# Query and key products of a two-stage attention: Strassen blocks of two heads by two batches in place of two heads by two halves of one batch

## The reference, cut to what matters

```python
qh = (q_in @ wq + bq).reshape(b, q_len, H, K)      # H = 16, K = 128, b = 4, q_len = 256, D = 256
kh = (kv_in @ wk + bk).reshape(b, t, H, K)         # kv_in is the same context in both
vh = (kv_in @ wv + bv).reshape(b, t, H, K)
kh = jnp.concatenate([kh, jnp.broadcast_to(bias_k, (b, 1, H, K))], axis=1)   # 257 keys
vh = jnp.concatenate([vh, jnp.broadcast_to(bias_v, (b, 1, H, K))], axis=1)
scale = jnp.sqrt(jnp.asarray(K, q_in.dtype))
logits = jnp.einsum('bqhk,bthk->bhqt', qh, kh) / scale
weights = jax.nn.softmax(logits, axis=-1)
ctx = jnp.einsum('bhqt,bthk->bqhk', weights, vh).reshape(b, q_len, H * K)
return ctx @ wo + bo
```

## Time and profile before

| what | us |
|---|---|
| median of 3 runs | 1529.41 (1529.25 to 1532.53) |
| the profiled execution, its own time | 1532.75 |
| its span, first to last instruction | 1529.90 |
| first wide stage | 258.76 to 634.94 |
| second wide stage | 634.94 to 1012.92 |
| TensorE / VectorE / ScalarE / GpSimd busy | 1460.5 / 978.5 / 938.6 / 208.2 |
| mean granted TensorE clock | 0.995 |

### The profile page before, as it was taken

One profiled execution on the slowest core, in us unless ns is written; L12 is line 12 of the kernel. 1 busy time (PEld: TensorE's weight loads), 2 busy tenths in 40 slices (PEclk: granted clock), 3 DMA queues, 4 the chain that ended last, 5 costly groups with the idle time before them and its releaser, 6 DMA issues.

```text
span 1529.9 us, 30796 instructions
## 1 busy us (share of the span) xinstructions
PE 1460.5 (95%) x10544; PEld 1144.6 (75%) x10544; DVE 978.5 (64%) x3454; ACT 938.6 (61%) x3047; POOL 208.2 (14%) x283
## 2 busy tenths in 40 slices
PE   7999999999999999999999999999899998999997
PEld 5766678888888888778878888878666666866664
DVE  4777822565565656556556665631899996158997
ACT  5878933544454444344445444533899997379996
POOL 2010042010010102201000010011222322012200
PEclk9999999999999999999999999999999999999999
DMA  7000002010010100101001000000100100000000
GB/s 297 1 2 2 35 31 80 32 39 26 1 62 3 49 16 1 63 1 49 16 1 63 1 1 1 7 9 1 56 2 9 36 16 8 1 1 9 16 2 22
DMA packets 10891, 40.79 MB, mean 27 GB/s; under 512 B 2417, under 2 KB 2673, under 8 KB 8689
## 3 DMA queue, kind: packets, MB, share of 16 engines
q1 hardware_dynamic: 10736, 38.82, 7.0%
HBM read 37.77 MB, written 1.05 MB: 25 GB/s over the span
## 4 chain that ended last, share of the span: by engine, by line
PE 64%; ACT 18%; issue 5%; DVE 2%; POOL 1%; POOLq 0%; DVEq 0%; ACTq 0%
ACT probs L1094 11%; PE bank L908 8%; PE bank L876 7%; PE bank L889 7%; PE bank L922 7%; PE bank L853 7%; PE bank L866 5%; PE bank L797 5%; ACT pT L1102 5%; PE bank L786 5%; PE bank L897 4%; PE bank L631 2%; PE bank L615 1%; PE bank L937 1%; ACT hT L1050 1%
## 5 line engine op out<-in xcount | busy, mean ns | idle before, releaser
L1094 ACT ACTIVATE probs<-probs,negmax 128x256 f32<-128x256 f32 (+1 forms) x640 | 351.8, 567 | 41.2 <-DVE negmax L1378 40.5
L1170 ACT ACTIVATE pT<-bank,cols 128x128 f32<-128x128 f32 x480 | 151.3, 372 | 247.0 <-PE bank L853 247.0
L631 PEld LDWEIGHTS bank<-ident,probs 128*128 128x128 f32 x1536 | 167.6, 141 | 119.5 <-ACT probs L1094 60.6
L631 PE MATMUL bank<-ident,probs 128*128 128x128 f32 x1536 | 226.1, 280 | 28.8 <-ACT pT L1102 17.5
L1378 DVE CUSTOM_DVE_ANT_0 probs<-bank,mask_a 128x256 f32<-128x256 f32 (+1 forms) x384 | 173.9, 509 | 28.5 <-PE bank L615 23.7
L1102 ACT ACTIVATE pT<-bank 128x512 f32<-128x512 f32 x288 | 172.9, 602 | 6.7 <-PE bank L631 6.6
L1523 DVE TENSOR_REDUCE stats<-bank 128x1 f32<-128x257 f32 x256 | 108.5, 425 | 74.7 <-PE bank L889 73.8
L1569 DVE TENSOR_TENSOR pT<-bank,pT 128x256 f32<-128x256 f32 x180 | 76.0, 422 | 118.4 <-PE bank L866 118.4
L1188 ACT ACTIVATE pT<-bank 128x512 f32<-128x512 f32 x128 | 76.5, 598 | 122.1 <-PE bank L897 122.1
L908 PE MATMUL bank<-pT,probs 128*128 128x256 f32 x512 | 139.9, 396 | 4.3 <-ACT pT L1188 4.1
L1094 ACT ACTIVATION_READ_ACCUMULATOR probs<-probs,negmax 128x1 f32 x640 | 138.1, 216 | 0.0
(11 more groups left out here) (198 smaller groups left out, 2680.0 us busy)
## 6 DMA issues: line engine op xcount, KB each, us to landing
w_m<-in_w SPq DMA_DIRECT2D x6, 1024.0 KB, 6.9
g_qkv<-in_g SPq DMA_DIRECT2D x4, 1536.0 KB, 6.8
q_res<-in_g SPq DMA_DIRECT2D x4, 1536.0 KB, 6.4
w_qkv<-in_w SPq DMA_DIRECT2D x3, 768.0 KB, 4.3
g_bv<-in_gbv SPq DMA_DIRECT2D x8, 256.0 KB, 6.7
g_o<-in_go SPq DMA_DIRECT2D x4, 512.0 KB, 3.4
q_res<-in_go SPq DMA_DIRECT2D x4, 512.0 KB, 3.2
rows<-in_rows SPq DMA_DIRECT2D x1, 1664.0 KB, 14.0
```

The costliest lines, as they stand in the source:

```text
L631: last = nc.tensor.transpose(out[:, n * P:(n + 1) * P], probs[:, u % PROBS, q * T + t * P:q * T + (t + 1) * P], ident[:, :])
L1094: last = nc.scalar.activation(s, s, ACT.Exp, bias=negmax[:, u % PROBS, k:k + 1], scale=-1.0, accum_out=sums[:, tile % 2, q, j * c.res + r: ...
L1170: last = nc.scalar.activation(to[:, w, :], bank[KQ_BANK][:, w * P:(w + 1) * P], ACT.Identity, bias=col(("bq", "bk")[w] + str(j), at))
```

## The change

A block is now two heads by two batches. Its halves in the third direction are two whole batches of 256 columns, where they were two halves of 128 columns of one batch. A block still has 7 products for query and 7 for key, each now 256 columns wide, and makes four heads-of-a-batch. There are 16 blocks a stage, of which two (8 heads-of-a-batch, `DIRECT`) are plain `kq`. Block steps run in rows 1 to 56, one step a row: in three rows of four `add_r1` and `add_r2` together ahead of `times_v`, in one row `add_r1` alone; none at the row's end. ScalarE reads one whole bank a row, VectorE adds one whole bank in three rows of four, behind `outputs(n)`. The ring has twelve places: five in pT, seven in `v_two`, which is therefore zeroed again behind the stages. `c_sum`'s second part lies in `w_qkv[0]`, so the load of that tile moves to the end of the second stage. The diff, cut to its core:

```diff
...
-PAIRS = HEADS // 2
-DIRECT = 4
...
+BLOCKS = HEADS // 4
+DIRECT = 8
...
-        qk1 = pT[:, 4:9, :].rearrange("p a t -> p (a t)")[:, 0:4 * (T + K1)].rearrange("p (n t) -> p n t", n=4)
-        h_sum = [m[:, i, :].rearrange("p (s t) -> p s t", s=4) for m in (mask_a, mask_m) for i in range(2)]
-        n = 4 * K1 + 2048
-        c_sum = [v_four[:, i, :, :, :].rearrange("p a b c -> p (a b c)") for i in range(2)] + [
-            pT[:, 9, :], flat[:, n:n + 512]]
-        c_sum = [x.rearrange("p (s t) -> p s t", s=4) for x in c_sum]
+        wide = [pT[:, 4:10, :].rearrange("p a t -> p (a t)"), v_two[:, :, :, :, :].rearrange("p a t r d -> p (a t r d)")]
+        qk1 = [wide[i >= 5][:, (i - 5 * (i >= 5)) * (T + K1):(i - 5 * (i >= 5) + 1) * (T + K1)] for i in range(12)]
+        h_sum = [m[:, :, :].rearrange("p i t -> p (i t)") for m in (mask_a, mask_m)]
+        c_sum = [v_four[:, :, :, :, :].rearrange("p i a b c -> p (i a b c)"),
+                 w_qkv[0][:, :, :, :].rearrange("p w k d -> p (w k d)")[:, 0:4 * T]]
+        h_sum, c_sum = [[x.rearrange("p (s t) -> p s t", s=4) for x in y] for y in (h_sum, c_sum)]
         q_all = g_qkv[0][:, :, :, :].rearrange("p w k d -> p (w k d)")[:, 0:2 * KT * T]
         q_all = q_all.rearrange("p (x i t) -> p x i t", x=2, i=KT)
...
+        def steps_in(n):
+            c = (n - 1) // 4 + DIRECT // 4
+            return (c, (n - 1) % 4) if n >= 1 and c < BLOCKS else None
+        def block_of(n):
+            u, h = divmod(n, H1)
+            return u // 2 * 2 + h // 2, (h % 2) * 2 + u % 2
+        def qk_of(n):
+            c, at = block_of(n)
+            return qk1[c % 3 * 4 + at]
...
-            load(w_qkv[0][:, :, :, :], a["w_2c"], "s_w0")
...
-            sp.wait_ge(sem("b_r1"), end("b12", "b_r1"))
+            sp.wait_ge(sem("b_r2"), end("b12", "b_r2"))
+            load(w_qkv[0][:, :, :, :], a["w_2c"], "s_w0")
...
-                    out = bank[SUM_BANK if n == 2 else KQ_BANK]
+                    out = bank[SUM_BANK if n >= 2 and n % 2 == 0 else KQ_BANK]
                     if n == 0:
                         weights("c_qkv", g, 16)
-                        rows_turned(pe, before, b)
                         pe.wait_ge(sem("b_r1out"), st.at("b_r1out", 0))
                     elif n == 2:
                         pe.wait_ge(sem("b_r2out"), st.at("b_r2out", 0))
-                    pe.wait_ge(sem("b_kq"), st.at("b_kq", 0, n - 1 if n == 3 else n if n < 2 else 1))
+                    if h == 0:
+                        rows_turned(pe, before, b)
+                    pe.wait_ge(sem("b_kq"), st.at("b_kq", 0, n - 1 if n >= 3 else min(n, 1)))
                     for k in range(KT):
                         mm(out[:, 0:T], g_qkv[g % 2][:, 1, k, h * P:(h + 1) * P], ctxT[:, b, k, :],
...
+                def blocks(c, w):
+                    g, bp, x, _ = block_at(c)
                     src = ctxT if w else hT
-                    return (lambda h, k: g_qkv[g % 2][:, w, k, at[h]], lambda s: w_sum[:, x, s - 1, w, :],
-                            lambda k, t: src[:, b, k, t * P:(t + 1) * P],
-                            lambda s: (c_sum if w else h_sum)[b][:, s - 1, :])
...
+                def add_r1(c, step):
+                    g, bp, x, i = block_at(c)
                     pe.wait_ge(sem("b_r1out"), st.at("b_r1out", 0, 4 * i + step))
                     if step == 0 and i == 0:
                         pe.wait_ge(sem("b_kq"), st.at("b_kq", 0, DIRECT))
-                    if step == 0 and b == 0 and x == 0:
+                    if step == 0 and bp == 0 and x == 0:
                         weights("c_qkv", g, 16)
                     if step == 0 and g == 0 and x == 0:
-                        rows_turned(pe, before, b)
+                        rows_turned(pe, before, 2 * bp)
                     if step == 1:
                         pe.wait_ge(sem("b_wsum"), st.at("b_wsum", 0, 2 * g + x + 1))
-                        pe.wait_ge(sem("b_hsum"), st.at("b_hsum", 0, B if g else b + 1))
+                        pe.wait_ge(sem("b_hsum"), st.at("b_hsum", 0, B // 2))
                         if i == 0:
-                            pe.wait_ge(sem("b_csum"), B)
+                            pe.wait_ge(sem("b_csum"), B // 2)
                     for w in range(2):
-                        wt, ws, xt, xs = blocks(m, w)
+                        wt, ws, xt, xs = blocks(c, w)
                         one, two = [(wt(0, 0), xt(0, 0)), (ws(2), xs(2)), (ws(3), xs(3)), (wt(1, 1), xs(4))][step]
-                        last = mm(bank[KQ_BANK][:, w * P:(w + 1) * P], one, two, start=(step == 0 and w == 0),
+                        last = mm(bank[KQ_BANK][:, w * T:(w + 1) * T], one, two, start=(step == 0 and w == 0),
                                   stop=(step == 3), skip_group_check=True)
                     last.then_inc(sem("b_r1"), 1)
...
+                def add_r2(c, step):
+                    i = block_at(c)[3]
                     pe.wait_ge(sem("b_r2out"), st.at("b_r2out", 0, 3 * i + step))
                     if step == 0 and i == 0:
                         pe.wait_ge(sem("b_kq"), st.at("b_kq", 0, DIRECT))
                     for w in range(2):
-                        wt, ws, xt, xs = blocks(m, w)
+                        wt, ws, xt, xs = blocks(c, w)
                         one, two = [(wt(0, 1), xt(1, 0)), (ws(1), xs(1)), (ws(4), xt(1, 1))][step]
-                        last = mm(bank[SUM_BANK][:, w * P:(w + 1) * P], one, two, start=(step < 2 and w == 0),
+                        last = mm(bank[SUM_BANK][:, w * T:(w + 1) * T], one, two, start=(step < 2 and w == 0),
                                   stop=(step != 1), skip_group_check=True)
                     last.then_inc(sem("b_r2"), 1)
...
-                        i = pair(n // 2)[3]
-                        pe.wait_ge(sem("b_r1out"), st.at("b_r1out", 0, 4 * (i + 1)))
-                        pe.wait_ge(sem("b_r2out"), st.at("b_r2out", 0, 3 * (i + 1)))
+                        c, at = block_of(n)
+                        i = block_at(c)[3]
+                        if at == 2:
+                            pe.wait_ge(sem("b_r1out"), st.at("b_r1out", 0, 4 * (i + 1)))
+                        else:
+                            pe.wait_ge(sem("b_r2out"), st.at("b_r2out", 0, 3 * i + (1, 3, None, 2)[at]))
...
-                kq(2)
-                kq(3)
+                for n in range(2, DIRECT):
+                    kq(n)
                 for n in range(HEADS):
-                    m = n // 2 + DIRECT // 2
                     u, h = divmod(n, H1)
                     if n + 1 < HEADS:
                         scores(n + 1)
...
-                    if n % 2 == 0:
-                        if n and m <= PAIRS:
-                            add_r2(m - 1, 2)
-                        if m < PAIRS:
-                            add_r1(m, 0)
-                    elif m < PAIRS:
-                        add_r1(m, 2)
-                        add_r2(m, 1)
+                    if steps_in(n):
+                        c, step = steps_in(n)
+                        add_r1(c, step)
+                        if step != 1:
+                            add_r2(c, max(step - 1, 0))
...
-                    if m < PAIRS:
-                        if n % 2 == 0:
-                            add_r1(m, 1)
-                            add_r2(m, 0)
-                        else:
-                            add_r1(m, 3)
...
+                def read_r1(c, step):
+                    g, bp, x, i = block_at(c)
                     act.wait_ge(sem("b_r1"), st.at("b_r1", 0, 4 * i + step + 1))
                     h, t = [(0, 0), (0, 1), (1, 1), (1, 0)][step]
...
+                    to, at = qk1[c % 3 * 4 + 2 * h + t], g * H1 + 2 * x + h
+                    nc.scalar.activation(to[:, 2 * T:T + K1], col(f"key{j}", at), ACT.Copy)
                     for w in range(2):
-                        last = nc.scalar.activation(to[:, w, :], bank[KQ_BANK][:, w * P:(w + 1) * P], ACT.Identity,
-                                                    bias=col(("bq", "bk")[w] + str(j), at))
+                        last = nc.scalar.activation(to[:, w * T:(w + 1) * T], bank[KQ_BANK][:, w * T:(w + 1) * T],
+                                                    ACT.Identity, bias=col(("bq", "bk")[w] + str(j), at))
                     last.then_inc(sem("b_r1out"), 1)
...
+                    if steps_in(n):
+                        read_r1(*steps_in(n))
...
+                    if c.host and p == 0:
+                        dve.wait_ge(sem("s_zero"), 3)
...
+                    to = qk1[c % 3 * 4 + (0, 3, 1)[step]][:, 0:2 * T]
+                    v.tensor_tensor(to, bank[SUM_BANK][:, :], to, ALU.add).then_inc(sem("b_r2out"), 1)
...
-                    if n and n % 2 == 0 and m <= PAIRS:
-                        add_r2(m - 1, 2)
...
+                    if steps_in(n):
+                        c, step = steps_in(n)
+                        if step != 1:
```

(79 more changed lines are left out.)

32 lines of the change are left out of this document (7 added, 25 removed).

## The result

The changed kernel takes 1520.2 us (median of 4 runs, 1520.17 to 1520.21); the kernel before took 1529.6 beside it (4 runs, 1529.25 to 1532.53). The ratio is 0.9933, with a 95% interval from 0.9921 to 0.9945. The forecast was 1521.5, with a range from 1517.0 to 1526.5. The profiled execution took 1520.21 with a span of 1518.4; the forecast for a profiled execution was 1524.8, from 1532.75 before.

The account below looks back on a forecast made before the run. Each stage was taken to last as long as TensorE's list. The terms summed to -7.9 us, taking the kernel's own 1532.75 to 1524.8; the median of the runs shown is 3.3 lower, so 1521.5, range 1517.0 to 1526.5.

Parts of the forecast that it names:

- Step products: TensorE's step records in both stages: fewer, 256-column records at 0.2156 us each, plus four more `kq`; -4.0 us.
- The wait for the turned block: 36 rows a stage: more step work behind the turns removes 0.07 us of waiting for ScalarE's copy; -5.0 us.
- rows with one sum: Rows h = 2, with `add_r1` alone: 0.03 us of saved step work returns as a wait in 28 rows; +0.8 us.
- VectorE before `values`: Rows h = 2: VectorE's `add_r2` no longer precedes the value add, so TensorE's second `values` stops waiting; -1.9 us.
- Row 0: First row: falls from 5.68 to 3.13 us, with its 12 step records counted elsewhere; -2.4 us.
- Rows 57 to 59: Both stages' rows left without step work: 0.96 us idle behind the turns in place of 0.07; +5.3 us.
- Row 60: Loses four records behind the turns and waits as much longer; +0.8 us.
- GpSimd, -1.5: Ahead of stage one: two 256-column `c_sum` replace four, shortening TensorE's 3.01 us idle before the next norm; -1.5 us.
- The clock: Falls to 1.2 GHz, about 1.7 us each: first may go (-1.7), both stage ends get thinner (+1.7 each); let cancel.
- Rival 5: Slower: `SUM_BANK` drained too late by VectorE, each of 112 step rows paying the excess; 1538 at 0.15 a row; chance 0.06.

Follow-up runs that it names:

- step_records_of_128: Changed kernel with every 256-column step product issued as two records of 128 columns, in both sums; 1527.2 us, ratio 0.9976.
- r2_at_row_end: Changed kernel with TensorE's second sum (`add_r2`) moved from behind the turned block to the row's end; 1527.9 us, ratio 0.9982.
- late_second_sum: Changed kernel with the last block's `add_r2` of steps 1 and 2 moved from rows 55 and 56 to 57 and 58; 1516.9 us, ratio 0.9911.
- late_sum_and_norm: Changed kernel with the last block's two late `add_r2` moved two rows later and GpSimd's next norm ahead of its second weight sum; 1515.9 us, ratio 0.9906.
- extra_adds_beside_none: Changed kernel with two needless VectorE adds ahead of each real one, only for a block's first and second sums; 1520.6 us, ratio 0.9935.
- norm_before_weights: Changed kernel with GpSimd's power and bias of the next norm ahead of stage one's second weight sum; 1518.55 us, ratio 0.9923.

## Why the prediction was right

It was right by its terms, not by luck between them; the sum for the two stages without the clock was -6.4 (-7.9 less GpSimd's -1.5), and the stages show -3.16 and, with the fall taken out, -3.4: together -6.6.

- **Step products, -4.0.** Records start 0.216 apart, as the nearest rows had it, and the unit of four rows went from 22.15 to 21.69 where 22.1 and 21.6 were forecast. `step_records_of_128` puts 2.54 a stage on the other side. The Trainium skill ("TensorE: Matmul & The Clock Gate", section "Wait — 56ns, not 53.3ns?") has columns over clock plus some 2.5 ns. The prediction tacitly took two clocks for each column of an fp32 record; counted so, the 256-column records agree with it (0.216, where it gives 0.2158), the 128-column ones don't in either kernel (0.1112 and 0.1117, where it gives 0.1092), and the measurement decides.
- **The wait for the turned block, -5.0, and rows with one sum, +0.8.** Nothing lost with 1.73 of cover, 0.09 with 0.87. The prediction had 0 for the first and 0.10 for the second (0.07 as before and 0.03 given back). `r2_at_row_end` gives back 3.3 a stage.
- **VectorE before `values`, -1.9.** The wait is gone and nothing took its place.
- **Row 0, -2.4.** 3.16 us, forecast 3.13.
- **Rows 57 to 59, +5.3.** 2.25 us in place of 2.26, with the wait of 0.69 named. `late_second_sum` gives 0.82 a row back, forecast price 0.89.
- **Row 60, +0.8.** From the turns to the learned values' product it is 3.23 us both before and after (608.68 to 611.91): the four records that went were all given back as a wait.
- **GpSimd, -1.5.** The idle is 1.60 after 3.01: -1.4.
- **What was missed, +0.3 in stage one.** The turns of row 63 start at 621.31, 0.27 later than the records before them end, because VectorE's normalising ends at 621.25. Before, the same row had no gap, nor has it one in stage two after (993.30 to 994.16, just the 0.86 of work). That is the difference between the 3.16 and the 3.4 of the two stages.
- **The clock.** It was held to cancel: one fall gone at 222, one added at each stage's end. The first went, as thought possible; the stages' ends got none and lost the one at 635; another came at 1071. Of the 11.5 us between the spans, 8.0 are the terms above (6.6 in the stages, 1.4 ahead of them). The other 3.5 lie where the clock differs: 1.9 at the head (0.2 of it already at the very start), 1.8 at the start of stage two, and 0.2 given back in the rest, with the new fall. So the profiled time came out 4.6 below the forecast of 1524.8, while the median, which before was taken from runs 3.3 shorter than the profiled one, came out only 1.3 below. That the median came so near is in this part luck: the clock was to cancel and did not.

Rival 5, the late `SUM_BANK`, was priced by the wrong event. It named the bank but gave the cover as 1.7 us, by the maxima. In ordinary rows at least 1.2 us are there: a delay of that length cost nothing. But beside GpSimd's weight sums the real addition ends at 477.38 and TensorE wants the bank at 478.24: 0.86 us are left. These are the rows that decided, 12 of 112; in the change as made none of them waits.

## What to carry to other kernels

Price work that is moved under a latency by the differences of starts in two rows that differ in just that work; a gap of 0.07 us in 72 rows was in no list of waits of the kernel before, and it was the largest of this change's gains. When work is moved to cover a latency, look for rows that it leaves bare, and leave the last pieces there: two sums moved by two rows brought 3.3 us. When an operation is called hidden, list everyone who waits for it, and read each cover in the row where its engine is slowest, not in an ordinary one.

## What the runs showed of the hardware

**VectorE's normalising is slowed beside GpSimd.** Timeline after, VectorE and GpSimd:

```profile
469.80 0.62 DVE L1535 TENSOR_SCALAR probs<-probs,stats 128x257 f32<-128x257 f32 x2
...
474.56 1.64 DVE L1535 TENSOR_SCALAR probs<-probs,stats 128x257 f32<-128x257 f32 x2
474.59 0.72 POOL L1710 TENSOR_TENSOR kT<-q_res 128x256 f32<-128x256 f32 x1 [64.22 <-PE bank L878]
475.27 0.78 POOL L1711 TENSOR_TENSOR kT<-q_res 128x256 f32<-128x256 f32 x1
...
476.70 0.68 DVE L1567 TENSOR_TENSOR v_two<-bank,v_two 128x512 f32<-128x512 f32 x1
```

The pair takes 0.62 us alone and 1.64 while GpSimd adds, whereas the addition that reads a bank takes 0.68 in both cases. In both stages of this trace 15 pairs take 1.00 to 1.65, each beside one of GpSimd's sums of 256 columns; no pair that runs alone is slow, nor are the six beside GpSimd's power of 128x2 (0.62). The Trainium skill ("SBUF — State Buffer", section "Who interferes with whom") states that a `tensor_scalar` of VectorE may take a pair of ports that it shares with GpSimd, and that one of the two then stands until the other's instruction is done, while an instruction with one input in SBUF outside those modes doesn't contend. The trace agrees in both, the loss of 1.02 us being a little more than one of GpSimd's instructions of 0.72 to 0.78; in which of its modes the `tensor_scalar` ran, no run here shows, and no run moved GpSimd's sums to see the pair go back to 0.62.

**The clock falls at other places in kernels that differ by little.** The table above has none to four before the end. A fall lasts about 3.4 us at 1.2 GHz and costs about 1.7 where TensorE sets the pace, and less in the rest behind the stages, where TensorE idles more: without a fall there it takes 515.28 (`late_sum_and_norm`), with one 516.20 (`extra_adds_beside_none`; 516.98 before), with two 516.95 to 517.80, and with three, of which one is at its first record, 517.83 (`norm_before_weights`). Runs of one kernel can lie in steps of about that size: on one chip the kernel before gave 1528.8 to 1529.2 five times, 1530.5 to 1530.8 five times and 1531.3 to 1532.1 four times. On another chip its 14 runs, from 1528.6 to 1532.8, show no such gaps. That the steps are numbers of falls is argued from the profiled executions; no more than one execution of a kernel was traced. Why a fall moves wasn't found: as said, the same 2.09 us of idleness precede it in one kernel and stay without it in another, and row 0 and the bare rows, which precede some, don't precede those at 1071 and 1344. For a change worth less than 3 us the lengths of the stages are a better measure here than the median.
